# A graph network in one kernel: indirect gathers and scatters on two semaphores that take turns, at most two in flight

## The reference

```python
# layer 0: tensor product of the source's row with the edge's harmonics, summed by node
x = segment_sum(messages0(x[src], sh0, sh1, sh2, W), dst)
# layer 1: two Chebyshev layers (order 3, so two sums over the graph in each), then attention
def cheb(x):
    unn = lambda f: segment_sum((f * dinv)[src], dst) * dinv
    X1 = -re_norm * unn(x) + x * (re_norm - 1)
    X2 = -2 * re_norm * unn(X1) + 2 * (re_norm - 1) * X1 - x
    return leaky_relu(concat(x, X1, X2) @ W + b)
h = cheb(cheb(x))
e = leaky_relu(fs[src] + fd[dst], 0.2)
a = softmax_by_dst(e @ attn)
x = leaky_relu(segment_sum(fs[src] * a, dst))
# layer 2: another tensor product, weights from a small network of the edge, gates
x = segment_sum(messages2(x[src], x[dst], edge_vec, emb, W1, W2) * norm, dst)
# layer 3: a plain sum of the sources' rows
x = segment_sum(x[src], dst)
```

## Time and profile before

| | |
|---|---|
| median of 3 runs | 14233.94 us |
| the profiled execution | 14251.11 us |
| its span in the trace | 14249.4 us |
| mean granted TensorE clock | 0.69 |

### The profile page before, as it was taken

One profiled execution on the slowest core, in us unless ns is written; L12 is line 12 of the kernel. 1 busy time (PEld: TensorE's weight loads), 2 busy tenths in 40 slices (PEclk: granted clock), 3 DMA queues, 4 the chain that ended last, 5 costly groups with the idle time before them and its releaser, 6 DMA issues. The chain is left out here.

```text
span 14249.4 us, 190118 instructions
## 1 busy us (share of the span) xinstructions
PE 5679.9 (40%) x81726; PEld 5084.1 (36%) x81726; DVE 5165.3 (36%) x5508; ACT 2179.3 (15%) x3067; POOL 7827.9 (55%) x7341
## 2 busy tenths in 40 slices
PE   1000000000000039588888600000002989999679
PEld 0000000000000039587887500000002877888568
DVE  4555555611000000101110122222222999999711
ACT  0100110100000000000000011111101555555300
POOL 5556655677667640311111267777766778888330
PEclk6555555555555569898999755555555999999889
DMA  3434434400000039586888421111111111111168
GB/s 117 144 124 145 148 124 141 153 3 7 0 20 8 4 111 359 210 316 250 309 316 302 143 46 33 39 33 39 33 24 20 40 33 43 44 40 40 36 244 333
DMA packets 532855, 1628.28 MB, mean 114 GB/s; under 512 B 249048, under 2 KB 331472, under 8 KB 440976
## 3 DMA queue, kind: packets, MB, share of 16 engines
q1 hardware_dynamic: 212928, 1145.92, 22.0%
q0 software_dynamic: 234368, 154.18, 5.7%
q10 hardware_dynamic: 84816, 316.94, 5.7%
HBM read 1265.79 MB, written 355.70 MB: 114 GB/s over the span
## 5 line engine op out<-in xcount | busy, mean ns | idle before, releaser
L215 POOL DMA_INDIRECT z_l<-table,idx_l x1568 | 1950.9, 1244 | 591.7 <-issue 495.0
L215 POOL DMA_INDIRECT g_l<-table_l,idx_l x1568 | 1626.8, 1038 | 1044.0 <-DMA s<-in_edge_w 563.8
L215 POOL DMA_INDIRECT g_gat<-table,idx_gat x1568 | 1621.5, 1034 | 562.7 <-issue 544.7
L755 POOL DMA_INDIRECT adj<-worth,cell x1568 | 1553.5, 991 | 657.6 <-issue 616.7
L2075 PE MATMUL p_t<-prod,ident 128*128 128x192 f32 x9464 | 1751.9, 336 | 119.0 <-issue 59.1
L2075 PEld LDWEIGHTS p_t<-prod,ident 128*128 128x128 f32 x9464 | 1541.0, 192 | 186.5 <-issue 123.9
L629 PE MATMUL acc_cheb0a<-parts_cheb0a,cells_cheb 128*128 128x96 bf16 x12348 | 627.5, 208 | 1931.5 <-issue 1177.8
L629 PEld LDWEIGHTS acc_cheb0a<-parts_cheb0a,cells_cheb 128*128 128x128 fp8e3 x12348 | 558.4, 98 | 2001.8 <-issue 1246.0
L1739 PE MATMUL pr<-diag,ones 128*128 128x256 f32 x2 | 1.2, 713 | 2232.4 <-DVE diag L1757 2232.4
L2343 DVE TENSOR_TENSOR prod<-p_t,h_l 128x768 f32<-128x768 f32 x784 | 744.4, 949 | 228.0 <-remote 143.1
L1739 PEld LDWEIGHTS pr<-diag,ones 128*128 128x128 f32 x2 | 0.5, 309 | 2232.7 <-DVE diag L1757 2232.7
(11 more groups left out here) (470 smaller groups left out, 10925.5 us busy)
## 6 DMA issues: line engine op xcount, KB each, us to landing
cells_cheb<-adj SPq DMA_DIRECT2D x560, 1344.0 KB
adj<-zeros ACTq DMA_DIRECT2D x28, 7056.0 KB
cells_l<-adj SPq DMA_DIRECT2D x140, 1344.0 KB
cells_cheb<-adj SPq DMA_DIRECT2D x56, 672.0 KB
gat_rows<-prod_gat ACTq DMA_DIRECT2D x28, 952.0 KB
g_l<-table_l,idx_l POOLq DMA_INDIRECT x1568
start_rows<-zeros ACTq DMA_DIRECT2D x28, 896.0 KB
scanned_rows<-msg_l ACTq DMA_DIRECT2D x28, 896.0 KB
```

The source lines that it names most:

```text
L215: return pool.indirect_dma_start(out=dest, out_offset=None, in_=table_ap, in_offset=bass.IndirectOffsetOnAxis(ap=index, axis=0))
L755: pool.indirect_dma_start(out=adj, out_offset=bass.IndirectOffsetOnAxis(ap=cell[:, t:t + 1], axis=0), in_=worth[:, t:t + 1].bitcast(U8), i ...
```

## The change

The three hardware loops over pairs of chunks are written out, chunk by chunk. The two semaphores of each place no longer stand for even and odd chunks but take turns DMA by DMA: DMA t adds to number t mod 2 (`lane_of`). Ahead of DMA t, from the third on, POOL waits until DMA t-2 has landed (`lane_free`), so at most two are in flight. Whoever waited for a chunk's 56 gathers on one semaphore now waits on both. In `scatter_cells` the wait after each chunk goes; `scattered` is counted ahead of the second DMA of the next chunk, after that DMA's own wait. `chunks_begun` goes. `CH` is `C_MSG` = 56, `GRP` is 56 too.

```diff
@@ -84,6 +84,8 @@
     LAST_C = ROUNDS[-1][0]
     assert NJ % RUN == 0 and all((c * 171) >> 11 == c // RC for c in range(CHUNKS))
     SLOTS = 4
+    BATCH = 1
+    assert C_MSG % (2 * BATCH) == 0
     TX = HL + T + HR
     assert TX % GRP == 0 and P * BT <= 32 * P and C_MSG == GRP
     HEAD, NEXT, PAUSE = 4 * GRP, 4 * GRP + 24, 20 * GRP
@@ -181,11 +183,10 @@
         keys_made = signal("keys_made")
         cells_put = signal("cells_put")
         cells_turned = signal("cells_turned")
-        adj_out = [signal(f"adj_out{b}") for b in range(2)]
+        adj_out = [signal(f"adj_out{k}") for k in range(2)]
         scattered = signal("scattered")
         fetched = [signal(f"fetched{k}") for k in range(BLOCKS)]
         s_scatter = signal("s_scatter")
-        chunks_begun = signal("chunks_begun")
         s_tp = signal("s_tp")
         s_xt = signal("s_xt")
         s_mm = signal("s_mm")
@@ -209,7 +210,16 @@
         stored = [signal(f"stored{b}") for b in range(2)]
 
         def gather_signals(tag):
-            return [signal(f"gathered_{tag}{b}") for b in range(2)]
+            return [signal(f"gathered_{tag}{k}") for k in range(2)]
+
+        def lane_of(lanes, t):
+            return lanes[t // BATCH % 2]
+
+        def lane_free(pool, lanes, t):
+
+            n = t // BATCH
+            if t % BATCH == 0 and n >= 2:
+                pool.wait_ge(lanes[n % 2], 16 * BATCH * (n // 2))
 
         def row_gather(pool, dest, table_ap, index):
             return pool.indirect_dma_start(out=dest, out_offset=None, in_=table_ap,
@@ -751,16 +761,16 @@
         def scatter_cells(pool, cell, worth, first, last):
 
             for t in range(first, last):
-                c = t // GRP
+                lane_free(pool, adj_out, t)
+                if t % GRP == BATCH and t > GRP:
+                    pool.sem_inc(scattered, 1)
                 pool.indirect_dma_start(out=adj, out_offset=bass.IndirectOffsetOnAxis(ap=cell[:, t:t + 1], axis=0),
                                         in_=worth[:, t:t + 1].bitcast(U8), in_offset=None, bounds_check=CELLS - 1,
-                                        oob_is_err=False).then_inc(adj_out[c % 2], 16)
-                if c and t % GRP == GRP - 1:
-                    pool.wait_ge(adj_out[(c - 1) % 2], 16 * GRP * ((c - 1) // 2 + 1))
-                    pool.sem_inc(scattered, 1)
-                if t == T - 1:
-                    pool.wait_ge(adj_out[c % 2], 16 * GRP * (c // 2 + 1))
-                    pool.sem_inc(scattered, 1)
+                                        oob_is_err=False).then_inc(lane_of(adj_out, t), 16)
+            if last == T:
+                for lane in adj_out:
+                    pool.wait_ge(lane, 8 * T)
+                pool.sem_inc(scattered, 1)
 
         def l0_pass(lo_f, hi_f, cell, worth):
             CH = C_MSG
@@ -940,12 +950,12 @@
                         nc.gpsimd.memset(zero_b[:], 0.0)
                         nc.gpsimd.affine_select(out=lower[:], in_=ones[:], compare_op=ALU.is_ge, fill=0.0,
                                                 base=0, pattern=[[1, P]], channel_multiplier=-1).then_inc(s_pool, 1)
-                        with pool.Fori(0, n) as i:
-                            for b in range(2):
-                                pool.wait_ge(loaded[b], at(loaded[b], 64 * (i + 1)))
-                                pool.sem_inc(chunks_begun, 1)
-                                for t in range(CH):
-                                    row_gather(pool, rows[b][:, t, :], table_l0, idx[b][:, t:t + 1]).then_inc(gathered[b], 16)
+                        for c in range(n_chunks):
+                            b = c % 2
+                            pool.wait_ge(loaded[b], at(loaded[b], 64 * (c // 2 + 1)))
+                            for t in range(CH):
+                                lane_free(pool, gathered, c * CH + t)
+                                row_gather(pool, rows[b][:, t, :], table_l0, idx[b][:, t:t + 1]).then_inc(lane_of(gathered, c * CH + t), 16)
                         pool.wait_ge(adj_zero, 16 * n_chunks)
                         pool.wait_ge(cells_turned, 32)
                         scatter_cells(pool, cell, worth, 0, HEAD)
@@ -969,7 +979,8 @@
                             g = rows[b]
                             w3, w4, w5 = (g[:, :, k:k + 24].rearrange("p t (o k) -> p t o k", k=3) for k in (40, 64, 88))
                             v_k = v_p.rearrange("p t (a k) -> p t a k", a=1).to_broadcast([P, CH, M, 3])
-                            v.wait_ge(gathered[b], 16 * CH * (times + 1))
+                            for lane in gathered:
+                                v.wait_ge(lane, 8 * CH * (c + 1))
                             scalars, vectors = acc_edge[:, :, 0:M], acc_edge[:, :, M:D].rearrange("p t (o k) -> p t o k", k=3)
 
                             def add(what, op=ALU.add):
@@ -1568,12 +1579,12 @@
 
                     @block.gpsimd
                     def _(pool):
-                        with pool.Fori(0, n) as i:
-                            for b in range(2):
-                                pool.wait_ge(idx_in[b], 16 * (i + 1))
-                                pool.sem_inc(chunks_begun, 1)
-                                for t in range(CH):
-                                    row_gather(pool, rows[b][:, t, :], table, idx[b][:, t:t + 1]).then_inc(gathered[b], 16)
+                        for c in range(2 * n):
+                            b = c % 2
+                            pool.wait_ge(idx_in[b], 16 * (c // 2 + 1))
+                            for t in range(CH):
+                                lane_free(pool, gathered, c * CH + t)
+                                row_gather(pool, rows[b][:, t, :], table, idx[b][:, t:t + 1]).then_inc(lane_of(gathered, c * CH + t), 16)
 
                     @block.vector
                     def _(v):
@@ -2031,12 +2043,12 @@
                     @block.gpsimd
                     def _(pool):
                         row_gather(pool, fill[:], table, first_row[:]).then_inc(s_agg, 16)
-                        with pool.Fori(0, n) as i:
-                            for b in range(2):
-                                pool.wait_ge(idx_in[b], 16 * (i + 1))
-                                pool.sem_inc(chunks_begun, 1)
-                                for t in range(CH):
-                                    row_gather(pool, z[b][:, t, :], table, idx[b][:, t:t + 1]).then_inc(gathered[b], 16)
+                        for c in range(NC):
+                            b = c % 2
+                            pool.wait_ge(idx_in[b], 16 * (c // 2 + 1))
+                            for t in range(CH):
+                                lane_free(pool, gathered, c * CH + t)
+                                row_gather(pool, z[b][:, t, :], table, idx[b][:, t:t + 1]).then_inc(lane_of(gathered, c * CH + t), 16)
 
                     @block.tensor
                     def _(pe):
@@ -2172,7 +2184,8 @@
 
                         def take(c, b, times, first=False):
 
-                            act.wait_ge(gathered[b], 16 * CH * (times + 1))
+                            for lane in gathered:
+                                act.wait_ge(lane, 8 * CH * (c + 1))
                             if not first:
                                 act.wait_ge(t_used, (c - 1) * PRS)
                             A.activation(zsf[:, :, 0:M], z[b][:, :, 0:M], ACT.Copy)
```

## The result

The changed kernel took 14367.4 us (median of 4 runs, 14365.78 to 14464.91), the kernel before, on the same chip, 14239.45 (4 runs): a ratio of 1.0103, interval 1.0056 to 1.0151. It is slower by 1.0%, clear of the noise though a small loss; the forecast was faster. In this text the step is the time from one launch of an indirect DMA to the next, the cap is the number of DMAs that POOL allows in flight, and PE is called starved where it has its data and yet issues only one matmul per launch or two.

A forecast was written before the change was run, and what follows sets the result against it. It held that steady indirect-DMA launches every 1.25 to 1.40 us starve instruction issue on other engines. Terms 27 + 44 + 24 - 270 - 196 = -371 gave 13,880 us (13,863 on the median's scale), range 13,460 to 14,680.

The forecast's parts named there:

- The step of the scatters: Scatter stage: launches 1.40 us apart under the new wait; +62, with the boundaries +24 us, ends -76 and +1035.
- Layer 0's cover: Layer 0: no direct cost, as POOL has 563.8 us of waiting to give; freed consumers give -196 us.
- The relief in the dense pass: First dense pass: matmuls that follow the scatters come earlier, beside them; -270 us, at most -370.
- signs of being right: New profile: POOL steps near 1.40, thousands of matmuls in the scatter stage, under 484 us after it, DVE's "remote" far under 640.9.
- Attention: Attention pass: 1568 gathers at 1.40 us, 2195 against 2168 us; +27, ends -200 and +184.
- Layer 2: Layer 2 gathers: only close pairs are stretched; +78 less 34 of slack, +44 us, ends -24 and +250.
- The slack of 34 us: End of layer 2: last gather starts at 13226.16, ACT takes its chunk only at 13260.53, some 34 us later.
- Written-out loops: Three gather stages: the hole at the second gather of each chunk pair might go; gain 0 to 24 us each.
- Rival 1: The wait binds and PE's starvation stays; step 1.50 gives +515, 14,749 us; middle 14,580; chance 0.38.
- mild form: The binding wait without relief at a step of 1.42 us: +59, +60 and +55, 14,408 us.
- Rival 2: Nothing binds: the wait is met before its turn, launches stay at 1.25 us; about -40, 14,195 us; chance 0.15.
- Rival 3: The hole comes at every change of semaphore, so every DMA: steps near 2.70 to 3.00, some +6600, 20,800 us; chance 0.03.

The follow-up runs named there:

- second pair: The kernel before and the changed kernel, both unchanged, run again on another chip: 12,473 us and 14,020 us, ratio 1.1231.
- one filler: Kernel before with one short GpSimd memset after each scatter from 672 to 1119, two after each from 1120 on: 14,129 us against 14,256.

## Why the prediction was wrong

By its own steps, on the chip it was made for: -371 forecast, +117 measured between the two traces. The terms missed by +426 (scatters), +189 (layer 0), -156 (dense pass), +12 (attention) and +22 (layer 2); the small rest lies between the stages.

- **The step of the scatters** is the one that failed: 1.40 taken, +24 for the stage; 1.51 to 1.79 measured, +450. I took today's step as the price of the wait, between bounds of 1.35 and 2.06, instead of asking what the scatter's own round trip is. The rows at hand were a start 2.69 us after the one before and 4.12 in the starved stretch. Half of the first is 1.35; the run at a cap of one gives 2.94, so 1.47. More than half of the excess is late landings while cells are loaded: 138 scatters at 3.3 us instead of 1.47 are some 247 us of the 450. No row of the kernel before could show that, since PE took almost no cells then: what the change freed collides with what it slowed.
- **Layer 0's cover.** "No direct cost, since POOL has 563.8 us of waiting to give", and -196 for freed consumers: measured -7. The waiting was given, all of it, to landings. That gathers there land late beside the writes of zeros stood in no row that I used; the cap of two makes every late landing a hole. Of the relief that I put at half, the second pair shows what is there: 2692 against 2151 us in the two conditions of one program.
- **The relief in the dense pass** was right in kind and too small: -270 taken, -426 measured (577 to 151), beyond the -370 that I called the most. That it came at all was luck by my own numbers. I forecast a step of 1.40, and at 1.39 the cap of three leaves PE starved with 543 matmuls; the relief came with landings that were late beside PE's own loads and spread the launches to 3.3 us, which the forecast did not have. Of my signs of being right, the thousands of matmuls and the vanished "remote" of DVE came true; POOL's step near 1.40 held in the attention alone (1.71 in layer 0, 1.67 in the scatters without their pauses, 1.69 in layer 2).
- **Attention** +27 taken, +39 measured: 1.41 against 1.40. **Layer 2** +44 taken; +106 in its gathers and -40 in what follows, +66. (The lower end of the attention should read -208, 1568 x 1.25 against 2168, not -200.) The slack of 34 us was real: ACT takes the last chunk 2.5 us after the last launch (13383.76 to 13386.22).
- **Written-out loops**: the holes stayed, 0 gained, as the row spoke against the rule.
- **Rival 1** (slower) had the side and not the mechanism: "the starvation stays". It went. The measured 14,367 lies near its mild form, 14,408, by chance. **Rival 2** fell with 2.94 and 2.6 against 2.57 and 2.50; by the Trainium skill's 2.0 us ("DMA: Bandwidth & Descriptors", Anatomy of one DMA) a cap of two would allow 1.0, and the traces show 1.3 to 1.5. From launch to landing they agree roughly with it (2.15 us for a scatter, 2.38 for a gather), and the next launch comes 0.78 or 0.26 us after the landing. **Rival 3** fell: no hole at each change of semaphore.
- **What the sum rested on.** I took the starved issue for a property of this kernel. It is one of where or when it runs: four of six later sets don't have it, and there the change costs 12.3% (measured in one of the four). Nothing in one trace could show that; I should have called it a condition that the forecast depends on. What sets it is open. The six later sets ran on six chips and none was seen in both conditions, so chip and moment aren't told apart.

## What to carry to other kernels

Before capping the DMAs in flight, measure launch to landing to next launch with a cap of one, and keep the cap times the issuing engine's own step clear of it, also where other traffic makes landings late: here 2.6 to 2.9 us and over 5 beside large writes, so two was too few, and four cost 0.8% in the scatters. Waiting time that an engine has to spare is only spare if what the change adds is paid from the same stretch. When one engine's issue looks starved by another's stream, run the same program elsewhere before building on it, and slow the stream with idle work first; with the packet records beside it, one run tells a rate from a count.

## What the runs showed of the hardware

- The same program takes 12.46 to 12.48 thousand us in four sets and 14.20 to 14.26 thousand in three (with the first pair). In the slower condition PE, while indirect DMAs are launched every 1.25 to 1.41 us, does about one matmul per launch or two (35 beside 71 launches in the kernel before, 65 beside 71 with one filler), and in the scatters never more than two are in flight then. It is free at a steady 1.9 to 2.0 with up to four in flight, and in the changed kernel at a mean of 3.3. The limit lies between 1.41 and 1.9; what the mechanism is stays open. The dense passes without such a stream are slower there too (2426 against 2144 us from the first sum's scatter to the attention), which the cap did not change (2422).
- A gather beside writes of 7 MB landed so late that the launch two behind it waited 4.6 us; without those writes the longest such wait was 2.5 us instead of 4.7 and layer 0's mean step 1.54 us instead of 1.71. A scatter beside the loads of cells has its last packet 5.2 us after its launch (median), and 1.75 us where nothing else moves.
- The 114th gather of a stage, and each 112th after it, comes some 3 us after the one before instead of 1.25, in loops and in written-out code (7403.30 to 7406.25), and also where the semaphores change at every DMA. Why is open.
